# Two shared-expert stages written out without loops, with 7 and 9 chunks in place of 8 and 8, places read directly by GpSimd, and a combination in rings of eight units

## The chip, the cores and the metric

The kernel runs on one core of a Trainium2 chip. The metric is the device time of one execution in microseconds; the table below gives the median of three runs. TensorE multiplies, VectorE and ScalarE work element by element, GpSimd issues the indexed transfers and some small arithmetic, SyncE issues plain transfers.

## What is computed

A layer over x of 4 x 2048 rows of 256 columns: a local attention with 31 taps, then a feed-forward part, each with a layer norm before and after and a residual.

```python
x = x + _layernorm(attn(_layernorm(x)))
y = _layernorm(x)
shared = silu(y @ sg.T) * (y @ su.T) @ sd.T * sigmoid(y @ shared_gate_w.T)     # 704 hidden columns
rw, sel = top_k(softmax(y @ gate_w.T), 2); rw = rw / rw.sum(-1)                # 16 experts
expert_out = sum over the 2 chosen of rw * (silu(g) * h) @ w_down              # 128 hidden columns each
out = x + _layernorm(expert_out + shared)
```

## The kernel before

The 8192 rows are 64 tiles of 128 rows. The program is a row of blocks with a barrier between them.

**Attention and routing** end with scratch tensors in HBM: the normed rows (`yn_scratch`), the same rows turned (`ynt_scratch`), the residual (`x2_scratch`); and in SBUF, for each row, its two places in the list sorted by expert (`slots`), its two shares and the sigmoid of the shared gate (`shgate`). At the end of routing, blocks of `sorted_rows` are cleared by SyncE and ScalarE.

**First shared stage** (`shared_and_scatter`). The shared expert runs over eight chunks of 512 rows (four tiles). A chunk has six steps m, one for each 128 hidden columns (the last has 64). All products are done in three terms of high and low parts. TensorE in step m does `gate_up` (L904) for step m + 2 and `down` (L915) for step m. ScalarE does `silu`: the silu of the gate (L861, waits for gate_up) and then the high part of the hidden values (L863, waits for VectorE). VectorE does `gated` (L886) and `hidden_low` (L891). `split_high` (L855) and `split_low` (L878) cut the chunk's input in two parts; `leave` (L869) brings the four finished tiles out of PSUM. Beside it GpSimd scatters every row to its two places (L984): 128 indexed transfers, 64 rows' tiles by two places, which read `sl`, a copy of a part of `slots` that VectorE makes (L1023). SyncE loads the rows, the transposed chunks (L817), the 16 experts' weights, two a chunk, and stores the shared result (L968). ScalarE and VectorE cut the experts' weights in high and low parts.

**Experts** (`experts`). 144 blocks of 128 sorted rows go through TensorE (L1119 turn, L1143 gate and up, L1150, L1157 down). SyncE loads the blocks (L1096) and stores the results to `expert_rows` (L1101); ahead of its loop it issues four block loads, eight tiny stores (L1106) and the two transposed chunks for the next stage (L817).

**Last stage** (`shared_and_combine`). Eight more chunks of the shared expert. Beside them the 64 tiles are combined in groups of four, in two streams: v = 0 takes the first 32 tiles, whose shared result is loaded back, v = 1 the tiles of the chunk just left. GpSimd gathers the expert rows (L1270, 128 indexed transfers in all). VectorE adds them with their shares and takes the moments (`sums`, L1343, L1347, L1351, L1354). GpSimd makes scale and shift (`scales`, L1277, L1278, L1281 a power, L1283). ScalarE applies them (`centred`, L1301), VectorE adds the residual (`finish`, L1361), SyncE stores (L1254). GpSimd's order is gather(0), gather(1), and then in a loop scales(0, i), gather(0, i + 1), scales(1, i), gather(1, i + 1).

Every engine works in the order of its own program. Waits are on semaphores that another engine counts up.

## Time and profile before

| | us |
|---|---|
| median of 3 runs | 1117.34 |
| lowest and highest | 1115.47, 1120.06 |
| the profiled execution | 1115.37 |
| its span | 1113.6 |

| engine | busy us | share of the span |
|---|---|---|
| TensorE | 950.6 | 85% |
| VectorE | 800.7 | 72% |
| ScalarE | 564.7 | 51% |
| GpSimd | 490.2 | 44% |

In rows of the profile PE is TensorE, DVE VectorE, ACT ScalarE, POOL GpSimd, SPq the queue of SyncE; L904 is line 904 of the kernel before. A row of the timeline is: start in us from the span's start, duration in us, engine, line, operation, out<-in, count, and in brackets the idle time of the engine before it and what ended it. The names of the tiles of the first shared stage begin with `s_`, those of the last with `c`.

### The profile page before, as it was taken

The page shows a single profiled execution, that of the slowest core. Times are in us where ns is not written, and L with a number is a line of the kernel's source. Part 1 is how long each engine was busy: PE and PEld are TensorE (multiplying, and loading weights), DVE is VectorE, ACT ScalarE, POOL GpSimd, SP SyncE. Part 2 cuts the span into 40 slices and gives each one's busy share as a digit, 9 for nine tenths or more (in the row PEclk, how much of TensorE's full clock was granted, in tenths as well). Part 3 has the DMA queues.
Part 4 walks back from the last instruction along what each step waited for, and adds up shares of the span by engine and source line. Part 5 has one row for each costly group of instructions (what it writes and reads, how often), then busy time and mean ns, then how long its engine had stood idle before and what let it go on. Part 6 is the DMA issues. An engine that isn't in the chain of part 4 may idle for free. (4 is left out here: it accounts for less than half of the span.)

```text
span 1113.6 us, 28049 instructions
## 1 busy us (share of the span) xinstructions
PE 950.6 (85%) x9192; PEld 838.9 (75%) x9193; DVE 800.7 (72%) x2066; ACT 564.7 (51%) x1309; POOL 490.2 (44%) x726
## 2 busy tenths in 40 slices
PE   5997898998899407999999589999998899898871
PEld 4787787876788405888888589998998787777761
DVE  5988997797998694444444278887887478777755
ACT  5992456995354313444444345555554345444432
POOL 4413556220555333767776200000000677787774
PEclk9998998999999557999999789999999899999995
DMA  4333688432678527656665345555554556665553
GB/s 137 118 106 92 199 235 263 151 117 65 165 212 248 181 98 242 202 190 208 225 202 180 118 150 170 172 173 175 165 174 151 152 152 189 186 184 168 164 169 109
DMA packets 188966, 188.16 MB, mean 169 GB/s; under 512 B 55120, under 2 KB 169936, under 8 KB 188752
## 3 DMA queue, kind: packets, MB, share of 16 engines
q1 hardware_dynamic: 173088, 149.25, 44.1%
q0 software_dynamic: 12288, 33.57, 9.1%
q10 hardware_dynamic: 3504, 4.20, 1.2%
q8 instruction: 53, 0.87, 0.3%
q14 instruction: 33, 0.27, 0.1%
HBM read 100.81 MB, written 86.14 MB: 168 GB/s over the span
## 5 line engine op out<-in xcount | busy, mean ns | idle before, releaser
L984 POOL DMA_INDIRECT sorted_rows<-yr,sl x128 | 138.1, 1079 | 75.7 <-issue 38.0
L1270 POOL DMA_INDIRECT cy<-expert_rows,csl x128 | 137.9, 1077 | 45.2 <-issue 44.0
L605 PE MATMUL bank<-xbd,am 128*32 128x68 f32 x4096 | 138.2, 304 | 11.2 <-DMA xbd<-xn_scratch 6.8
L605 PEld LDWEIGHTS bank<-xbd,am 128*32 128x32 f32 x4096 | 122.7, 128 | 18.7 <-issue 8.8
L1263 POOL MEMSET czero<- 128x4 f32 x1 | 0.1, 103 | 241.3 <-POOLq L1049 241.3
L886 DVE TENSOR_TENSOR s_hf<-s_sg,bank 128x512 f32<-128x512 f32 (+1 forms) x48 | 33.0, 688 | 89.1 <-ACT s_sg L861 89.1
L1143 PE MATMUL bank<-eh,xh 128*128 x288 | 94.5, 328 | 0.5 <-DVE xl L1187 0.5
L1187 DVE TENSOR_TENSOR xl<-bank,xh 128x256 fp32r<-128x256 f32 x144 | 61.1, 425 | 40.8 <-ACT xh L1169 33.2
L1169 ACT ACTIVATE xh<-bank 128x256 fp32r<-128x256 f32 x144 | 55.4, 385 | 65.3 <-PE bank L1119 64.9
L407 DVE TENSOR_TENSOR am<-probs,mask 128x512 f32<-128x512 f32 x128 | 80.0, 688 | 8.3 <-ACT probs L500 7.4
L1143 PE MATMUL bank<-el,xh 128*128 x288 | 82.3, 286 | 0.0
L1143 PE MATMUL bank<-eh,xl 128*128 x288 | 82.2, 285 | 0.0
L863 ACT ACTIVATE c_hh<-c_hf 128x512 fp32r<-128x512 f32 (+1 forms) x48 | 30.4, 632 | 97.8 <-DVE c_hf L886 97.8
L915 PE MATMUL bank<-dh,c_hh 128*128 128x256 f32 (+1 forms) x192 | 57.1, 297 | 24.7 <-DVE c_hl L891 24.7
L1119 PE MATMUL bank<-ident,xg 128*128 128x128 f32 x288 | 57.2, 282 | 24.4 <-DMA xg<-sorted_rows 12.3
L904 PE MATMUL bank<-c_yh,gh 128*128 128x512 f32 x176 | 72.1, 410 | 6.4 <-DVE c_yl L878 6.4
L514 ACT ACTIVATE av<-av,shift,rstd 128x256 f32<-128x256 f32 x64 | 35.0, 594 | 81.7 <-POOL shift L327 81.7
L322 POOL TENSOR_TENSOR rstd<-mv,eps 128x2 f32<-128x2 f32 (+1 forms) x68 | 14.3, 210 | 138.5 <-DVE mv L397 83.3
L904 PE MATMUL bank<-s_yh,gh 128*128 128x512 f32 x176 | 71.2, 405 | 4.5 <-DVE s_yl L878 4.5
L348 POOL TENSOR_TENSOR x<-av,xr 128x256 f32<-128x256 f32 x64 | 47.0, 755 | 62.8 <-ACT yn L523 59.4
L904 PE MATMUL bank<-c_yl,gh 128*128 128x512 f32 x176 | 70.9, 403 | 0.0
L904 PE MATMUL bank<-c_yh,gl 128*128 128x512 f32 x176 | 70.7, 402 | 0.0
(196 smaller groups left out, 3110.4 us busy)
## 6 DMA issues: line engine op xcount, KB each, us to landing
xg<-sorted_rows SPq DMA_DIRECT2D x144, 128.0 KB, 2.1
expert_rows<-yo SPq DMA_DIRECT2D x144, 128.0 KB, 1.8
xbd<-xn_scratch SPq DMA_DIRECT2D x128, 72.0 KB, 2.3
xt<-xp SPq DMA_DIRECT2D x32, 256.0 KB, 3.0
xn_scratch<-xn SPq DMA_DIRECT2D x64, 128.0 KB, 2.8
xr<-x SPq DMA_DIRECT2D x32, 256.0 KB, 3.6
x_scratch<-x SPq DMA_DIRECT2D x32, 256.0 KB, 3.5
yn_scratch<-yn SPq DMA_DIRECT2D x32, 256.0 KB, 3.5
```

Source lines behind the costliest of these rows:

```text
L348: nc.gpsimd.tensor_tensor(x2[:, q, t], av[:, q, t], xr[:, q, t], ALU.add).then_inc(s["x2_ok"], 1)
L407: nc.vector.tensor_tensor(am[:, q, g], probs[:, bass.ds(i * CB, CB), g, None, :].to_broadcast([P, CB, 2, J]), mask[:, None].to_broadcast([ ...
L514: nc.scalar.activation(av[:, q, t], av[:, q, t], ACT.Identity, scale=rstd2[:, q, t:t + 1], bias=shift2[:, q, t:t + 1]).then_inc(s["z_ok"], 1)
L605: ins = nc.tensor.matmul(pso[q][t][J * b:J * b + J, g * MW:(g + 1) * MW], am[:, q, g, e, side], xbd[:, q, e + side, :, g], start=(g == 0 a ...
L904: ins = self.nc.tensor.matmul(self.pb[2 * k + half][:], w[:, c, col:col + P], y[:, q, c, :], start=(j == 0), stop=(j == 5))
L915: ins = self.nc.tensor.matmul(o, a[0:f, g, t * P:(t + 1) * P], w[0:f, m, :], start=(m == 0 and t % 2 == 0 and j == 0), stop=(m == FT - 1 a ...
L984: nc.gpsimd.indirect_dma_start(out=xg_d, out_offset=bass.IndirectOffsetOnAxis(ap=sl[:, q, t, u, k:k + 1], axis=0), in_=yr[:, t, u], in_off ...
L1119: ins = nc.tensor.transpose(px[r % 2][:, c * P:(c + 1) * P], xg[:, r, c * P:(c + 1) * P], ident[:])
L1143: ins = nc.tensor.matmul(pg[r % 2][:, 0:2 * MF], a[:, r % 2, c * P:(c + 1) * P], w[:, bass.ds(e, 1), c * C:(c + 1) * C], start=(j == 0), s ...
L1169: nc.scalar.activation(xh[:, r % 2], px[r % 2][:, 0:C], ACT.Copy).then_inc(s["xh_ok"], 1)
L1187: nc.vector.tensor_tensor(xl[:, r % 2], px[r % 2][:, 0:C], xh[:, r % 2].bitcast(F32), ALU.subtract).then_inc(s["xl_ok"], 1)
L1270: nc.gpsimd.indirect_dma_start(out=y[:, v, k, j], out_offset=None, in_=yg_d, in_offset=bass.IndirectOffsetOnAxis(ap=sl[:, v, k, j:j + 1], ...
```

## The change

The loops over chunks are written out, so all waits are for constants. The first shared stage takes 7 chunks, the last 9. GpSimd reads `slots` directly for its scatters and gathers; the copies on VectorE are gone. In the first stage SyncE loads two experts and then only rows; ScalarE issues the other experts' loads, the transposed chunks (those of the last stage's first two chunks too) and the stores of the shared result, which the last stage waits for. The low part of the 64 last hidden columns is put into the other half of the high part's tile, below weights that are repeated there, so `down` has two products a tile in place of three in that step.

In the last stage the tiles are combined in 32 units of two tiles. `order` is the sequence of the units, `sums_at` the step of VectorE at which each unit's sums stand: steps 2 to 5 of the first chunk, steps 0, 2, 3 and 5 of the next two, steps 2, 3 and 5 of the rest, and two units behind the last chunk. `centred` stands one step later in ScalarE's program, `finish` two steps later in VectorE's. All buffers of the combination have eight places. GpSimd's sequence is six gathers, then scales and gather in turn.

```diff
+CHUNKS = T // 512
+FIRST = 7
+LATER = CHUNKS - FIRST
...
+        low = self.hl[0:f, g] if m < FT - 1 else self.hh[FL:2 * FL, g]
...
+        terms = ((self.hh, self.dh), (self.hh, self.dl), (self.hl, self.dh))
+        if m == FT - 1:
+            terms = terms[0:2]
...
+            for e in range(2):
+                load_expert(sp, e)
+            for t in range(PAIRS):
+                if t >= R:
+                    sp.wait_ge(s[f"sc_out{t % R}"], t // R * 64)
+                sp.dma_start(yr[:, t % R], yn_d[2 * t:2 * t + 2].rearrange("t p c -> p t c")).then_inc(s[f"yr_in{t % R}"], 16)
...
-                            for k in range(TOPK):
-                                nc.gpsimd.indirect_dma_start(
-                                    out=xg_d, out_offset=bass.IndirectOffsetOnAxis(ap=sl[:, q, t, u, k:k + 1], axis=0),
...
+            for t in range(PAIRS):
+                po.wait_ge(s[f"yr_in{t % R}"], t // R * 16 + 16)
+                for u in range(2):
+                    for k in range(TOPK):
+                        nc.gpsimd.indirect_dma_start(
+                            out=xg_d, out_offset=bass.IndirectOffsetOnAxis(ap=slots[:, 2 * t + u, k:k + 1], axis=0),
+                            in_=yr[:, t % R, u], in_offset=None).then_inc(s[f"sc_out{t % R}"], 16)
...
+            def store(n):
+                act.wait_ge(s["so_ok"], n * 4 + 4)
+                act.dma_start(sh_d[n * 4:n * 4 + 4].rearrange("t p c -> p t c"), so[:]).then_inc(s_kept, 16)
+
+            sh.split_high(act, 0)
+            for n in range(FIRST):
                 for m in range(FT):
...
+                    sh.silu(act, n, m)
+                    if m == 0 and n + 1 < FIRST:
+                        sh.split_high(act, n + 1)
+                    if m == 2 and n > 0:
+                        leave(n - 1)
+                    if m == 4 and n > 0:
+                        store(n - 1)
+                    if m == 4 and n + 2 < CHUNKS:
+                        load_turned(act, sems, yt, ynt_d, n + 2)
+                    if (n, m) in turn:
+                        e = turn.index((n, m))
+                        act.wait_ge(s[f"e_in{e % 2}"], e // 2 * 16 + 16)
+                        nc.scalar.activation(eh[:, e:e + 1], eraw[:, e % 2:e % 2 + 1], ACT.Copy).then_inc(s["e_hi"], 1)
+                    if m % 2 == 1 and m + FT * n > 1 and (e := (m + FT * n + 1) // 2) < E:
+                        load_expert(act, e)
+            leave(FIRST - 1)
+            store(FIRST - 1)
...
-            for q in range(2):
-                load_turned(sp, sems, yt, ynt_d, SHARED_CHUNKS + q, q)
...
+    R, AHEAD = 8, 6
+    EARLY = FIRST * 2
+    MORE = EARLY - 4 - (LATER - 1)
+    order, sums_at, kept = [], {}, 0
+    for n in range(FIRST, CHUNKS):
+        for m in range(2, FT) if n == FIRST else (0, 2, 3, 5) if n - FIRST <= MORE else (2, 3, 5):
+            own = n > FIRST and m in (2, 3)
+            sums_at[n, m] = len(order)
+            order.append((n - 1) * 2 + m - 2 if own else kept)
+            kept += not own
+    order += [(CHUNKS - 1) * 2, (CHUNKS - 1) * 2 + 1]
+    UNITS = len(order)
+    place = {unit: i for i, unit in enumerate(order)}
+    steps = [(n, m) for n in range(FIRST, CHUNKS) for m in range(FT)]
+    finish_at = {steps[k + 2]: sums_at[at] for k, at in enumerate(steps) if at in sums_at and k + 2 < len(steps)}
+    centre_at = {steps[k + 1]: sums_at[at] for k, at in enumerate(steps) if at in sums_at and k + 1 < len(steps)}
...
+            def gather(i):
+                r, unit = i % R, order[i]
+                if i >= R:
+                    po.wait_ge(s["s2_ok"], (i - R) * 2 + 2)
+                for t in range(2):
                     for j in range(TOPK):
...
+                        nc.gpsimd.indirect_dma_start(out=y[:, r, t, j], out_offset=None, in_=yg_d,
+                                                     in_offset=bass.IndirectOffsetOnAxis(ap=slots[:, 2 * unit + t, j:j + 1], axis=0)
+                                                     ).then_inc(s[f"y_in{r}"], 16)
+
+            def scales(i):
+                r = i % R
+                po.wait_ge(s["mv_ok"], i * 2 + 2)
+                nc.gpsimd.tensor_tensor(rstd[:, r], mv[:, r, :, 1], eps[:, 0:2], ALU.add).then_inc(s["var_ok"], 1)
+                nc.gpsimd.tensor_tensor(shift[:, r], zero[:], mv[:, r, :, 0], ALU.subtract).then_inc(s["var_ok"], 1)
+                po.wait_ge(s["var_ok"], i * 2 + 2)
+                nc.gpsimd.tensor_tensor(rstd[:, r], rstd[:, r], neg_half[:, 0:2], ALU.pow).then_inc(s["dev_ok"], 1)
+                po.wait_ge(s["dev_ok"], i + 1)
+                nc.gpsimd.tensor_tensor(shift[:, r], shift[:, r], rstd[:, r], ALU.mult).then_inc(s["norm_ok"], 1)
+            for i in range(UNITS + AHEAD):
+                if i >= AHEAD:
+                    scales(i - AHEAD)
+                if i < UNITS:
+                    gather(i)
...
+            def leave(n):
+                at = [place[2 * n], place[2 * n + 1]]
+                if at[1] >= R:
+                    act.wait_ge(s["o_ok"], (at[1] - R) * 2 + 2)
+                sh.leave(act, n, lambda t: (ff[:, at[t // 2] % R, t % 2:t % 2 + 1], s["so_ok"]))
...
+            sh.split_high(act, FIRST)
+            for n in range(FIRST, CHUNKS):
                 for m in range(FT):
...
+                    sh.silu(act, n, m)
+                    if m == 0 and n + 1 < CHUNKS:
+                        sh.split_high(act, n + 1)
+                    if m == 1 and n > FIRST:
+                        leave(n - 1)
+                    if m == 3 and n + 2 < CHUNKS:
+                        load_turned(act, sems, yt, ynt_d, n + 2)
+                    if (n, m) in centre_at:
+                        centred(centre_at[n, m])
+            left = [i for i in range(UNITS) if i not in centre_at.values()]
+            leave(CHUNKS - 1)
+            for i in left:
+                centred(i)
...
+            def sums(i):
+                r, unit = i % R, order[i]
+                ve.wait_ge(s[f"y_in{r}"], (i // R + 1) * 64)
+                if unit < EARLY:
+                    ve.wait_ge(s[f"in{r}"], loads_of(i) * 16)
+                for t in range(2):
+                    k = 2 * unit + t
+                    if unit >= EARLY:
+                        ve.wait_ge(s["so_ok"], k - 2 * EARLY + 1)
+                    nc.vector.scalar_tensor_tensor(ff[:, r, t], y[:, r, t, 0], share[:, k:k + 1, 0], ff[:, r, t],
+                                                   ALU.mult, ALU.add).then_inc(s["s1_ok"], 1)
+                for t in range(2):
...
+            sh.split_low(ve, FIRST)
+            for n in range(FIRST, CHUNKS):
                 for m in range(FT):
...
+                    sh.gated(ve, n, m)
+                    if m == 1 and n + 1 < CHUNKS:
+                        sh.split_low(ve, n + 1)
+                    if (n, m) in finish_at:
+                        finish(finish_at[n, m])
+                    if (n, m) in sums_at:
+                        sums(sums_at[n, m])
+                    sh.inner_low(ve, n, m)
+            for i in range(UNITS):
+                if i not in finish_at.values() and i not in sums_at.values():
+                    sums(i)
+            for i in range(UNITS):
+                if i not in finish_at.values():
+                    finish(i)
...
-    dn = np.concatenate([i["L0_ffn_shared_w_down"].T, np.zeros((FT * P - FF, C), "f")], 0)
+    dn = np.concatenate([i["L0_ffn_shared_w_down"].T, i["L0_ffn_shared_w_down"].T[FF - FL:]], 0)
```

## Rows read from the trace of the kernel before

**Rows 1.** Stretches: us, busy PE, PEld, DVE, ACT, POOL, PEclk, DMA share, GB/s.
```profile
426.50:623.00 196.50, 196.50 (x1104) 169.46 (x1104) 88.39 (x150) 88.13 (x147) 138.06 (x128) 0.99 0.60 197
...
632.00:860.00 228.00, 210.45 (x1724) 206.01 (x1724) 178.53 (x574) 119.16 (x431) 0.00 (x0) 0.98 0.54 166
...
866.60:1084.00 217.40, 199.62 (x1080) 168.83 (x1080) 156.01 (x390) 97.44 (x182) 164.79 (x204) 0.97 0.56 173
1084.00:1113.60 29.60, 4.64 (x24) 4.13 (x24) 16.50 (x47) 8.18 (x17) 13.62 (x20) 0.60 0.35 110
```

**Rows 2.** The chain that ended last, by line, shares of the span.
```profile
POOL cy L1270 10%; PE bank L904 2%; POOL crstd L1281 2%; POOL crstd L1277 1%; PE bank L915 1%; POOL cshift L1278 0%; ACT cff L1301 0%; DVE cff L1347 0%; POOL cshift L1283 0%; DVE cff L1343 0%; DVE cst L1351 0%; ACT L1296 0%; DVE c_yl L878 0%; ACT c_yh L855 0%; DVE cmv L1354 0%
```

**Rows 3.** Timeline of GpSimd's scatters: first, one at the loop's back edge, last.
```profile
431.33 1.23 POOL L984 DMA_INDIRECT sorted_rows<-yr,sl  x1 [23.48 <-DMA yr<-yn_scratch]
...
476.50 0.97 POOL L984 DMA_INDIRECT sorted_rows<-yr,sl  x1 [2.27 <-DVE sl L1023]
...
619.74 1.90 POOL L984 DMA_INDIRECT sorted_rows<-yr,sl  x1 [0.30 <-issue]
```

**Rows 4.** Waits, first shared stage: total us, times, longest us.
```profile
POOL sorted_rows L984 <- DVE sl L1023: 13.9, 7, 2.3
```

**Rows 5.** The chain in order of time: one step's down products.
```profile
877.38 1.44 PE bank L915 x12
```

**Rows 6.** Timeline: last product of the first shared stage, ScalarE's first act in experts.
```profile
622.85 0.28 PE L915 MATMUL bank<-dh,s_hl 64*128 64x256 f32 x1
...
628.15 1.28 ACT L1165 ACT_TABLE_LOAD   x1 [3.35 <-PEq L936]
```

**Rows 7.** Timeline at the start of the experts: SyncE's queue and TensorE.
```profile
633.96 0.98 SPq L817 DMA_DIRECT2D yt<-ynt_scratch  x2
634.98 3.80 SPq L1096 DMA_DIRECT2D xg<-sorted_rows  x5
...
641.68 0.69 PE L1119 MATMUL bank<-ident,xg 128*128 128x128 f32 x2 [4.99 <-DMA xg<-sorted_rows]
```

**Rows 8.** Stretches behind the hole, columns as in rows 1 (PEclk 1.00 is 2.4 GHz).
```profile
641.70:645.80 4.10, 4.10 (x20) 4.10 (x21) 1.76 (x6) 1.38 (x5) 0.00 (x0) 0.50 0.06 17
```

**Rows 9.** DMA issues: count, KB each, median us to landing.
```profile
xg<-sorted_rows SPq DMA_DIRECT2D x144, 128.0 KB, 2.1
```

**Rows 10.** Groups by line, GpSimd, last stage: busy us, mean ns, idle before.
```profile
L1283 POOL TENSOR_TENSOR cshift<-cshift,crstd 128x4 f32<-128x4 f32 x16 | 4.4, 275 | 1.3
```

**Rows 11.** Timeline of GpSimd, last stage: gathers 1 and 16, period, loop's back edge.
```profile
864.20 1.00 POOL L1270 DMA_INDIRECT cy<-expert_rows,csl  x1 [1.17 <-DVE csl L1329]
...
885.25 0.95 POOL L1270 DMA_INDIRECT cy<-expert_rows,csl  x1 [0.30 <-issue]
...
897.08 1.02 POOL L1270 DMA_INDIRECT cy<-expert_rows,csl  x1 [0.60 <-issue]
...
923.57 0.36 POOL L1277 TENSOR_TENSOR crstd<-cmv,eps 128x2 f32<-128x2 f32 x2
...
1083.43 1.01 POOL L1270 DMA_INDIRECT cy<-expert_rows,csl  x1 [0.55 <-issue]
```

**Rows 12.** Timeline of ScalarE, last stage: silu of step 3, one centred group.
```profile
881.66 0.60 ACT L861 ACTIVATE c_sg<-bank 128x512 f32<-128x512 f32 x1 [2.25 <-PE bank L904]
...
906.05 2.07 ACT L1301 ACTIVATE cff<-cff,cshift,crstd 128x256 f32<-128x256 f32 x4
```

**Rows 13.** Timeline of VectorE, last stage: first sum, low part behind four sums, split.
```profile
887.13 0.88 DVE L1343 SCALAR_TENSOR_TENSOR cff<-cy,share,ckept 128x256 f32<-128x256 f32 x2
...
889.72 0.66 DVE L891 TENSOR_TENSOR c_hl<-c_hf,c_hh 128x512 fp32r<-128x512 f32 x1
...
910.58 1.21 DVE L878 TENSOR_TENSOR c_yl<-yt,c_yh 128x1024 fp32r<-128x1024 f32 x1
```

**Rows 14.** Timeline of the end: first operation of the last scales, last finish.
```profile
1105.45 0.34 POOL L1277 TENSOR_TENSOR crstd<-cmv,eps 128x2 f32<-128x2 f32 x2 [7.58 <-DVE cmv L1354]
...
1108.43 1.80 DVE L1361 TENSOR_TENSOR co<-cff,cx 128x256 f32<-128x256 f32 x4 [3.07 <-ACT cff L1301]
```

More of the change, by code:

```diff
@@ L919, in down, with products @@
             ins.then_inc(self.s["dn_full"], 1)
-    def products(self, pe):
-        def chunk(i, q, first=False, last=False):
-            if first:
-                self.gate_up(pe, i, q, 0)
-                self.gate_up(pe, i, q, 1)
+    def products(self, pe, lo, hi):
+        self.gate_up(pe, lo, 0)
+        self.gate_up(pe, lo, 1)
+        for n in range(lo, hi):
             for m in range(FT):
                 if m + 2 < FT:
-                    self.gate_up(pe, i, q, m + 2)
-                elif not last:
-                    self.gate_up(pe, i + 1, 1 - q, m + 2 - FT)
-                self.down(pe, i, q, m)
-        self.chunks(pe, chunk)
@@ L1034, in _, with expert_low @@
-            chunk(0, 0, first=True)
-            chunk(1, 1)
-            with ve.Fori(0, SHARED_CHUNKS // 2 - 2) as k:
-                chunk(k * 2 + 2, 0)
-                chunk(k * 2 + 3, 1)
-            chunk(SHARED_CHUNKS - 2, 0)
-            chunk(SHARED_CHUNKS - 1, 1, last=True)
+            def expert_low(e):
+                ve.wait_ge(s["e_hi"], e + 1)
+                nc.vector.tensor_tensor(el[:, e:e + 1], eraw[:, e % 2:e % 2 + 1], eh[:, e:e + 1].bitcast(F32),
+                                        ALU.subtract).then_inc(s["e_lo"], 1)
@@ L1042, in _ @@
+            sh.split_low(ve, 0)
+            for n in range(FIRST):
+                for m in range(FT):
+                    sh.gated(ve, n, m)
+                    if m == 2 and n + 1 < FIRST:
+                        sh.split_low(ve, n + 1)
+                    if m % 2 == 0 and 0 <= (e := (m + FT * n) // 2 - 1) < E:
+                        expert_low(e)
+                    sh.inner_low(ve, n, m)
         @block.tensor
         def _(pe):
-            sh.products(pe)
-def experts(nc, sems, eh, el, yt, ynt_d, first_d, xg_d, yg_d, ident, ones, block_expert, pb):
+            sh.products(pe, 0, FIRST)
@@ L1221, in shared_and_combine @@
-        zero = sb("czero", [P, G])
-        names = ["passed", "vpassed", "zeros", "kept_in"] + [f"{n}{v}" for v in range(2) for n in
-                 "sl_ok y_in x2_in s1_ok s2_ok st_ok mv_ok var_ok dev_ok norm_ok z_ok o_ok o_out".split()]
+        y = sb("cy", [P, R, 2, TOPK, C])
+        x2 = sb("cx2", [P, R, 2, C])
+        ff = sb("cff", [P, R, 2, C])
+        st = sb("cst", [P, R, 2, 6])
+        mv = sb("cmv", [P, R, 2, 2])
+        rstd = sb("crstd", [P, R, 2])
+        shift = sb("cshift", [P, R, 2])
@@ L1261, in _ @@
+            for r in range(R):
+                sp.wait_ge(s[f"o_out{r}"], UNITS // R * 16)
         @block.gpsimd
```

408 lines of the change are left out of this document (120 added, 288 removed).

## The prediction, as put on record before the result

> **What bounds the kernel now.** I read the stretches by stage first, then the chain that ended last, then the order of work on GpSimd at each end of the two shared stages. All times are microseconds of the profiled execution. The four lines of [rows 1] are the first shared stage, the experts, the last stage and its end. The shared expert's first stage is TensorE's: busy 196.5 of 196.5 [rows 1]. The experts are TensorE's but for one hole. The last stage is not TensorE's: it works 199.6 of 217.4, and another 29.6 follow in which it does little [rows 1]; the chain there is GpSimd's gathers [rows 2]. So there are three sums to make, and GpSimd's own length must be held against TensorE's in both shared stages.
>
> **First shared stage (8 chunks become 7).** TensorE loses a chunk: 8 chunks last from 426.5 to 623.1, 24.5 each [rows 1, 6]. The last block of hidden columns takes 8 products where it took 12; twelve take 1.44 [rows 5], so 0.5 per chunk goes. TensorE would end at 623.1 - 24.5 - 3.5 = 595. But GpSimd issues all 128 scatters in this stage: from 431.33 to 621.6 [rows 3]. What the change removes is the wait for the copies of places, 13.9 in seven waits of up to 2.3 [rows 4]; less the ordinary gap of 0.30 in each, 11.8. GpSimd then ends at 609.8 if it starts when it did. The first row load, which ends its first wait [rows 3], is now issued behind 0.79 MB of expert weights; at the 197 GB/s of the stage [rows 1] that is up to 4, I take 2, the middle (bounds 0 and 4): 611.8. TensorE is 17 ahead, so this stage is now bound by GpSimd, and the waits moved to ScalarE (expert and transposed loads, the store, which are behind its own casts) have that cover; without it they would cost their issue, some 0.5 each by SyncE's two in 0.98 [rows 7]. Before, the next stage's table load began at 628.15, 6.5 after GpSimd's end, because the last store had to land behind ScalarE's exit copies [rows 6]. Now the landing of a scatter (about 3) ends it: 614.8. **Gain 13.3, bounds 11 and 17.** The skewed queue of SyncE only carries rows now; each pair waits for the scatter four pairs back, which is 20 away, so it costs nothing.
>
> **Experts.** SyncE issued two 512 KB loads at 633.96 ahead of the fifth block's rows at 634.98; TensorE then stood still for 4.99 and ran at half clock from 641.7 to about 645.8 [rows 7, 8]. Both loads leave this queue. At full speed these 4.1 would be 2.1. **Gain 7.0**, bounds 4 (a late landing remains) and 7.5. Nothing takes the hole's place: rows of that size land in 2.1 [rows 9], and the load is issued about 2.7 before it is needed.
>
> **Last stage (8 chunks become 9).** By TensorE alone: one chunk more, 0.5 less in each. It isn't TensorE's stage, so I follow GpSimd. Its order is now: gather units 0 to 5 (four gathers each), then scales(0), gather 6, scales(1), and so on. ScalarE's centred(i) stands one step after sums(i) in ScalarE's own order and waits for scales(i); behind it on ScalarE are all later silu's, on which VectorE and TensorE wait. Call P(i) the time at which scales(i) is done.
>
> P(0): 16 gathers took 864.2 to 886.2, 1.38 each [rows 11]; 24 take 33. Starting at 863.3 (no copy of places to wait for) they end at 896.4, and scales(0) adds 1.4: for four tiles the set took 2.2 (from 1105.45 to 1108.43 less 0.8 of ScalarE and hand-overs [rows 14]), and one addition and one power of 0.7 together go. P(0) = 897.8. ScalarE reaches centred(0) after the silu of step 3, and that step's silu stands at 881.7 [rows 12]. So it stands still for some 14 in the first chunk.
>
> Period of GpSimd: between 897.08 and 1083.43 lie 13 sets of eight gathers and one scales of four tiles, 14.33 each [rows 11]. Two units have the same gathers and powers, one subtraction and one product more (0.28 each, by the product's row [rows 10]), one more pair of semaphore steps (0.15) and one more of the 0.55 gaps in place of 0.30 [rows 11]: 15.1; 0.2 of it were waits that go: 14.9, **7.45 a unit** (bounds 7.1 and 7.7).
>
> Spacing: sums stand at consecutive steps in chunks 8 to 10 in most places, and 7.45 rules there. Where the next sums stand two steps on, the path is centred 1.0 (four took 2.07) and silu 0.6 [rows 12], gated 0.6, finish 0.7, sums 2.6 [rows 13]: 5.5, just below what GpSimd needs for its four gathers (5.5 to 5.9): again 7.45. From the last sums of a chunk (step 5) to the next at step 2 there are three steps: first gated and the high cast of step 0 and the high split delay centred by about 1.2; then centred 1.0, silu 0.6, gated 0.6, low split 1.2 [rows 13], finish 0.7, low cast 0.6, gated 0.6, sums 2.6 = 7.9 (8.2 with the exit copies on ScalarE), then scales 1.4 and 0.2 of hand-overs: 11.0. So chunks with three units take 7.45 + 7.45 + 11.0 = 25.9, above TensorE's 24.
>
> Sum: P(11) = 897.8 + 11 x 7.45 = 979.8. P(12) = 990.8, P(14) = 1005.7, and four more chunks give P(26) = 1109.3. Behind P(26) (at step 0 of the last chunk): to P(27) 11; inner casts, sums 28, centred 27 and 28 to the last block's sums 10.5; last products and exit 2.5; sums of units 30 and 31, 5.5; scales 1.4, centred and finish 1.8, and the store: from the last sums' tiles at 1110.2 to the end at 1113.6 was 3.4 [rows 1, 14]. Together 36: end at 1145.3 instead of 1113.6. **Loss 31.7.** The two tiles per unit in the tail are already in it.
>
> **Total**: -13.3 - 7.0 + 31.7 = +11.4. The profiled execution took 1115.37 for a span of 1113.6 and lies 2 below the median 1117.34; applied to the median, 1128.7. The bounds of the period (21 periods of GpSimd's own) give -7 and +5, those of the first two stages -4 and +6: 1115 to 1141.
>
> **A rule of the Trainium skill against a row.** At the back edge of the scatter loop there is a gap of 2.27 [rows 3], and at that of the combining loop none: its first addition follows the gather at 923.57 without idle time [rows 11]. "Runtime: NRT & Kernel Launch", Instruction fetch mechanics, in the Trainium skill says that a taken branch whose target is out of the two pages held makes the engine wait for a fetch. By the rule, straight-line code would save such a wait at each back edge; the trace agrees for the first loop, and not for the second.
>
> **Rivals.**
> 1. GpSimd runs through. ScalarE's and VectorE's path never holds it, so P(26) = 897.8 + 26 x 7.45 = 1091.5 and the end 1127.5: loss 13.9, total -6.4, 1111. For it: two of three paths come out at or below GpSimd's period. Against: the three-step path is 3 above it. Chance 0.15.
> 2. TensorE rules the last stage. 9 chunks of 24 from 866.6 and 2.4 of slow start give 1085, some 10 of tail, 1095: total -39, 1078. That needs GpSimd to be done with 128 gathers and 32 scales by then, 237 from 863.3, so 1100: against. Chance 0.07.
> 3. Back edges. If GpSimd's loop of the last stage holds waits like the first loop's 2.27 in place of 0.30 [rows 3], hidden in the 14.33 per turn, six go, 12 less than the forecast: 1117. The addition without idle time at 923.57 [rows 11] speaks against. Chance 0.06. This is the rule of the page named above.
> 4. Slower than forecast and than before by another mechanism: TensorE's clock. In chunks 7 to 9 TensorE has 4.0 of work in 7.45. After 5 idle it ran at 1.2 GHz [rows 7, 8]; if it stays there, a step is 8 and rules over 7.45, and each restart lags: half a step (4) in each of three to five chunks, 12 to 20 more, 1144. It decides once a step at the lower clock exceeds GpSimd's period. Against: 4 of work brought the full clock back [rows 8]. Chance 0.10.
> 5. The change doesn't do what it says: scatters don't close up, because their transfers or rows hold them. Then the first stage gains 8 rather than 13.3: 1134. Chance 0.05.
>
> **How the numbers follow.** Forecast 0.57, its own range 1115 to 1141. The range of 8 in 10 takes in most of rivals 1, 3 and 5: 1102 to 1144. A measurement of this kernel tells 0.5%, 5.6, from no change. Faster by over that (under 1111.8): most of rival 1, rival 2, a little of the forecast's low end: 0.22. Within it (to 1122.9): rest of rival 1, rival 3, the forecast's lower part: 0.20. Slower: 0.58.
>
> **What would show it.** In the first stage GpSimd without waits of 2, ending near 611 with TensorE idle from 595; experts without the hole of 5; in the last stage ScalarE waiting some 14 for cshift before its fourth silu of the stage, waits of ScalarE on cshift in all chunks, additions every 7.45 on GpSimd and 11 once a chunk. The prediction is wrong if GpSimd waits for VectorE's moments in the first chunks (then it is ahead, and rival 2 comes near), or if ScalarE's waits on GpSimd are absent.

## Result and the profile after

| | before | after |
|---|---|---|
| median | 1116.62 (4 runs) | 1122.95 (4 runs, 1121.66 to 1125.45) |
| ratio, 95% interval | | 1.0056 (1.0035 to 1.0077) |
| span of the profiled execution | 1113.6 | 1119.9 |
| until ScalarE's table load that opens the experts | 628.15 | 616.95 |
| from there to the table load of the last stage | 234.8 | 234.0 |
| from there to the end | 250.7 | 269.0 |

The changed kernel is slower by 0.6%: small, but its interval leaves out 1. By stage the two profiled executions differ by -11.2, -0.8 and +18.3, together +6.3. The forecast had -13.3, -7.0 and +31.7.

The stretches of the kernel after, with the columns of [rows 1]: the first shared stage, the time until TensorE begins the experts, its first 11.7 there (two lines), the rest of the experts, the last stage and its end.

```profile
424.80:617.00 192.20, 164.44 (x938) 144.80 (x938) 78.43 (x107) 79.31 (x136) 141.40 (x128) 0.93 0.64 206
617.00:619.30 2.30, 0.04 (x1) 0.04 (x1) 0.00 (x0) 1.23 (x1) 0.00 (x0) 0.50 0.47 128
619.30:629.00 9.70, 8.32 (x36) 7.46 (x37) 3.38 (x10) 3.08 (x10) 0.00 (x0) 0.50 0.45 95
629.00:631.00 2.00, 2.00 (x13) 2.00 (x12) 0.94 (x3) 0.83 (x3) 0.00 (x0) 0.63 0.00 0
632.00:850.00 218.00, 200.97 (x1674) 197.64 (x1673) 174.31 (x561) 115.56 (x418) 0.00 (x0) 1.00 0.54 167
850.90:1092.00 241.10, 211.85 (x1124) 178.11 (x1125) 160.56 (x379) 106.99 (x197) 176.22 (x237) 0.96 0.56 164
1092.00:1119.90 27.90, 13.28 (x84) 11.65 (x82) 21.00 (x58) 11.15 (x22) 8.52 (x20) 0.79 0.17 57
```

TensorE is no longer busy throughout the first shared stage (164.4 of 192.2). The timeline there, GpSimd's first and last scatters, TensorE's first act in the experts and the table load, answers [rows 3] and [rows 6]:

```profile
432.85 1.56 POOL L959 DMA_INDIRECT sorted_rows<-yr,slots  x1 [25.27 <-DMA yr<-yn_scratch]
...
612.00 0.96 POOL L959 DMA_INDIRECT sorted_rows<-yr,slots  x1 [0.30 <-issue]
...
616.95 1.28 ACT L1136 ACT_TABLE_LOAD   x1 [24.65 <-PEq L929]
...
619.26 1.15 PE L1090 MATMUL bank<-ident,xg 128*128 128x128 f32 x4 [28.63 <-DMA xg<-sorted_rows]
```

GpSimd ends at 613.0, and TensorE had stopped 28.6 before its next product. The hole of [rows 7] is gone; at the same block TensorE now waits 0.83:

```profile
627.07 0.69 PE L1090 MATMUL bank<-ident,xg 128*128 128x128 f32 x2 [0.83 <-DMA xg<-sorted_rows]
```

The waits of the last stage (us in all, times, longest) show which engine is held up by which:

```profile
ACT c_hh L849 <- DVE c_hf L868: 78.2, 54, 3.5
...
ACT cff L1271 <- POOL cshift L1256: 54.6, 23, 12.2
POOL crstd L1251 <- DVE cmv L1320: 38.6, 12, 8.2
POOL cy L1244 <- issue: 34.9, 127, 0.3
PE bank L888 <- DVE c_hf L868: 17.9, 13, 8.1
```

Before, ScalarE waited for the shift (`cshift`) 10.9 in two waits, and GpSimd for VectorE's moments (`cmv`) 16.2 in three. After, ScalarE waits 54.6 and GpSimd 38.6: each holds the other up. The timeline of the first such wait, ScalarE's silu of step 3 and the first `centred`, and GpSimd's first shift:

```profile
869.64 0.60 ACT L847 ACTIVATE c_sg<-bank 128x512 f32<-128x512 f32 x1 [2.26 <-PE bank L888]
...
883.56 0.20 POOL L1256 TENSOR_TENSOR cshift<-cshift,crstd 128x2 f32<-128x2 f32 x1
...
883.79 1.09 ACT L1271 ACTIVATE cff<-cff,cshift,crstd 128x256 f32<-128x256 f32 x2 [12.17 <-POOL cshift L1256]
```

and, from the fourth chunk on, the scales of the first unit in a chunk with three units:

```profile
971.00 0.54 POOL L1251 TENSOR_TENSOR crstd<-cmv,eps 128x2 f32<-128x2 f32 x1 [3.92 <-DVE cmv L1320]
...
996.03 0.54 POOL L1251 TENSOR_TENSOR crstd<-cmv,eps 128x2 f32<-128x2 f32 x1 [3.92 <-DVE cmv L1320]
...
1021.06 0.54 POOL L1251 TENSOR_TENSOR crstd<-cmv,eps 128x2 f32<-128x2 f32 x1 [3.92 <-DVE cmv L1320]
```

The same wait of 3.92 comes back every 25.03, one chunk of three units. The path behind it goes from the last sums of a chunk (step 5) over three steps to the first of the next (step 2): there a chain that closes on itself sets the pace, and no engine alone. It does not make up all of the 38.6. In the chunks of four units GpSimd waits 0.48 at most and sets the pace itself, a unit every 7.0 to 7.5. Five waits of 2.65 to 3.93 stand at the first unit of chunks of three units (18.3 in all), two of 0.48 ahead of them, and the other 19.3 are five waits at the end, from 1095.30 on.

### The profile page after: what moved, and what is told of

The parts are those of the page before. It is cut to its first block and busy times, and to the rows that moved or that the text cites. A ratio compares the mean times of both kernels' runs of the same rounds, so it can differ in the third digit from the quotient of the medians.

```text
span 1119.9 us, 27085 instructions
## 1 busy us (share of the span) xinstructions
PE 940.7 (84%) x9128; PEld 833.6 (74%) x9129; DVE 796.3 (71%) x2018; ACT 564.6 (50%) x1309; POOL 497.7 (44%) x758
## 3 DMA queue, kind: packets, MB, share of 16 engines
q1 hardware_dynamic: 159120, 131.68, 38.7%
## 5 line engine op out<-in xcount | busy, mean ns | idle before, releaser
L959 POOL DMA_INDIRECT sorted_rows<-yr,slots x128 | 141.4, 1105 | 64.0 <-issue 38.4
L1244 POOL DMA_INDIRECT cy<-expert_rows,slots x128 | 133.8, 1046 | 35.6 <-issue 34.9
L888 PE MATMUL bank<-c_yh,gh 128*128 128x512 f32 x198 | 82.8, 418 | 24.2 <-DVE c_hf L868 17.9
L868 DVE TENSOR_TENSOR c_hf<-c_sg,bank 128x512 f32<-128x512 f32 (+1 forms) x54 | 37.0, 685 | 74.0 <-ACT c_sg L847 73.7
L888 PE MATMUL bank<-c_yl,gh 128*128 128x512 f32 x198 | 80.7, 407 | 0.0
L888 PE MATMUL bank<-c_yh,gl 128*128 128x512 f32 x198 | 80.5, 407 | 0.0
L868 DVE TENSOR_TENSOR s_hf<-s_sg,bank 128x512 f32<-128x512 f32 (+1 forms) x42 | 28.9, 688 | 67.9 <-ACT s_sg L847 67.9
L849 ACT ACTIVATE c_hh<-c_hf 128x512 fp32r<-128x512 f32 (+1 forms) x54 | 34.2, 633 | 78.2 <-DVE c_hf L868 78.2
L1090 PEld LDWEIGHTS bank<-ident,xg 128*128 128x128 f32 x288 | 35.9, 142 | 46.7 <-DMA xg<-sorted_rows 30.1
```

The lines of the kernel that those rows point to most:

```text
L868: self.nc.vector.tensor_tensor(self.hf[0:f, k], self.sg[0:f, k], up, ALU.mult).then_inc(self.s["hf_ok"], 1)
L888: ins = self.nc.tensor.matmul(self.pb[2 * k + half][:], w[:, c, col:col + P], y[:, n % 2, c, :], start=(j == 0), stop=(j == 5))
L959: nc.gpsimd.indirect_dma_start(out=xg_d, out_offset=bass.IndirectOffsetOnAxis(ap=slots[:, 2 * t + u, k:k + 1], axis=0), in_=yr[:, t % R, u ...
L1090: ins = nc.tensor.transpose(px[r % 2][:, c * P:(c + 1) * P], xg[:, r, c * P:(c + 1) * P], ident[:])
L1244: nc.gpsimd.indirect_dma_start(out=y[:, r, t, j], out_offset=None, in_=yg_d, in_offset=bass.IndirectOffsetOnAxis(ap=slots[:, 2 * unit + t, ...
```

## The experiments

All edit the changed kernel. The stages of each profiled execution, cut at the two table loads. In the last stage also three quantities of GpSimd: its waits for `cmv`, the busy time of its 128 gathers, and that of its small operations (`scales`).

| kernel | first | experts | last | waits cmv | gathers | small |
|---|---|---|---|---|---|---|
| before | 628.2 | 234.8 | 250.7 | 16.2 | 137.9 | 43.5 |
| after | 617.0 | 234.0 | 269.0 | 38.6 | 133.8 | 52.3 |
| three ahead | 618.8 | 232.7 | 260.7 | 29.3 | 135.2 | 52.4 |
| later steps | 619.3 | 231.8 | 252.0 | 9.3 | 137.6 | 62.1 |
| later steps, four ahead | 616.0 | 232.4 | 241.2 | 0 | 135.7 | 62.1 |
| 8 and 8 chunks | 620.3 | 230.7 | 255.4 | 26.5 | 132.0 | 52.7 |
| TensorE kept busy | 618.1 | 230.1 | 269.2 | 38.7 | 133.9 | 53.1 |
| loads back on SyncE | 617.2 | 237.0 | 269.7 | 38.6 | 134.4 | 53.1 |
| four ahead | 618.1 | 232.5 | 263.6 | 32.7 | 134.6 | 52.4 |
| later, four ahead, kept busy | 617.7 | 229.7 | 244.2 | 0 | 140.0 | 60.4 |
| the same, 8 and 8 | 636.2 | 230.0 | 233.9 | 0 | 136.2 | 54.5 |
| 8 and 8, later, four ahead | 621.8 | 231.0 | 234.4 | 0 | 136.7 | 54.1 |

Two things are read from it first. The first two stages have the same code after and in three ahead, four ahead, later steps, and later steps with four ahead, and yet the first ends between 616.0 and 619.3 and the experts take 231.8 to 234.0: single executions tell no less than 2 to 3 there. The last stage repeats better: its code is the same after, with TensorE kept busy and with the loads back on SyncE, and it took 269.0, 269.2 and 269.7. And in the last stage the sum of the three GpSimd columns moves as the stage does: from after to the version with later steps and four ahead it falls by 38.6 - 1.9 - 9.8 = 26.9, the stage by 27.8.

### The distance between gathers and scales

```diff
-    R, AHEAD = 8, 6
+    R, AHEAD = 8, 3
```

> The changed kernel with one number changed: GpSimd gathers three units ahead of the scales, not six. Theory A (the order of scales and centred sets the last stage: ScalarE waits in centred for scales, and a chunk of three units is a loop of 25): the first scales are done 12 gathers, not 24, after the stage's start, so about 10 to 15 earlier (VectorE's first moments then come last), and after that the cadence of 25 a chunk stays. The last stage is 10 to 14 shorter, the span near 1108. Theory B (GpSimd's total of gathers and scales is the bound, whatever the order): no change, 1120. Theory C (TensorE's ninth chunk): no change.

The last stage fell by 8.3, less than the 10 to 14 expected. Its waits:

```profile
ACT cff L1271 <- POOL cshift L1256: 43.8, 23, 4.5
...
POOL crstd L1251 <- DVE cmv L1320: 29.3, 11, 4.1
```

The wait of 12.2 is gone, the 23 waits are not: only what stood ahead of the first scales was removed. The scales of the second unit begin 11.8 earlier (877.02, 888.85 after), as expected, and those of unit 27 still 11.5. The rest is lost at the end: what is not gathered ahead at the start has to be gathered there, so that units 27 and 28 are 7.0 apart where they were 3.6 in the version with six ahead. A dose between the two, AHEAD = 4:

> The changed kernel with AHEAD 4 in place of 6 and nothing else; with AHEAD 3 alone the last stage fell by 8.3, with all later steps moved it fell by 17.0, and both together (AHEAD 4) by 27.8. Theory A (only the start counts: ScalarE's wait for the first scales and shift, 12.2 with six units ahead, is what shrinks; every later period is that of the path sums, scales, centred, which doesn't know how far the gathers run ahead): one unit more ahead than in the version with three, so one unit of four gathers, 5, later; the last stage falls by 3 to 6, span 1113 to 1117. Rival B (the gains add up, so AHEAD 4 by itself is worth 27.8 less 17.0): the last stage falls by about 10.8, span 1107 to 1110.

It fell by 5.4, as theory A had it. Two units fewer ahead than in after bring the first `centred` 9.6 earlier (874.21 here, 883.79 after), two units' gathers. The later pace doesn't change: the scales of unit 27 are 9.5 earlier too (1085.77 and 1095.30), and the same 7.0 in place of 3.6 behind them takes most of the difference to 5.4.

```profile
874.21 1.10 ACT L1271 ACTIVATE cff<-cff,cshift,crstd 128x256 f32<-128x256 f32 x2 [2.46 <-POOL cshift L1256]
```

### The distance between sums and centred

`centred` stands five steps behind `sums` in ScalarE's order in place of one, `finish` six in place of two, and the store on SyncE follows two units later.

```diff
-    finish_at = {steps[k + 2]: sums_at[at] for k, at in enumerate(steps) if at in sums_at and k + 2 < len(steps)}
-    centre_at = {steps[k + 1]: sums_at[at] for k, at in enumerate(steps) if at in sums_at and k + 1 < len(steps)}
+    finish_at = {steps[k + 6]: sums_at[at] for k, at in enumerate(steps) if at in sums_at and k + 6 < len(steps)}
+    centre_at = {steps[k + 5]: sums_at[at] for k, at in enumerate(steps) if at in sums_at and k + 5 < len(steps)}
```

> The changed kernel with centred five steps behind the sums instead of one, and finish six instead of two (SyncE's stores lag six units, not four). Order of GpSimd as in the changed kernel. Theory A: the waits of ScalarE for the scales nearly go, the loop of 25 per chunk becomes TensorE's 23.5, GpSimd runs on at 7.15 a unit without waiting for moments; a shift of about 14 stays, since scales lag six gathers. End of the last stage some 20 to 26 earlier: span 1094 to 1100. Theory B: GpSimd's 128 gathers and 32 scales from 851.7 last until 1080 in any order, with a tail of 10: 1090 to 1095 at the least, but it would have been the bound before too, so no gain over 4. Theory C: no change.

The last stage fell by 17.0; 20 to 26 were expected, so the size was missed. GpSimd's wait for the moments fell from 38.6 to 9.3, all of it in the tail, and ScalarE's for the shift from 54.6 to 28.2, of which 26.2 lie ahead of 960:

```profile
ACT cff L1271 <- POOL cshift L1256: 28.2, 10, 4.5
...
POOL crstd L1251 <- DVE cmv L1320: 9.3, 3, 5.4
```

Three terms stand against the gain. The 9.3: with six units gathered ahead, the scales of six are still to come when the last gather is issued, and the last ones wait for VectorE. Then 9.8 went into GpSimd's small operations, which became longer (table: 52.3 to 62.1), and 3.8 into its gathers. The edit moves `centred`, `finish` and the stores together; what each of the three is worth was not measured. With both edits and AHEAD = 4:

> As the run before, and GpSimd gathers four units ahead instead of six. Theory A: both causes of the wait are smaller; TensorE is late by some 5 only, the last chunk ends near 1074, the tail adds 12 to 16: span 1086 to 1092, faster than the kernel before by 2%. Theory B and theory C: as in the run before, no gain to speak of.

Median 1093.65 (1091.28 to 1096.47), ratio to before 0.980 (0.977 to 0.983), span 1089.6 as expected. The last stage fell by 27.8, more than the 17.0 and 5.4 of the parts, and the table shows where: the tail's 9.3 goes only when both are there. That is a reading of two waits, not an experiment of its own. The waits of its last stage have no line of GpSimd for `cmv`, and ScalarE's for the shift are nearly gone:

```profile
ACT cff L1271 <- POOL cshift L1256: 5.8, 5, 2.5
```

GpSimd works from its first gather at 849.13 to the end of its last scales at 1085.36, and its waits for other engines in these 236.2 are 0.6 in all; the rest of its idle time is gaps between its own instructions. Now it is the bound, of a stage of 241.2 in which TensorE is busy for 215.5. Its groups by line:

```profile
L1244 POOL DMA_INDIRECT cy<-expert_rows,slots x128 | 135.7, 1060 | 35.3 <-issue 34.0 <-POOL czero L1235 0.7 <-DVE cff L1313 0.6
...
L1252 POOL TENSOR_TENSOR cshift<-czero,cmv 128x2 f32<-128x2 f32 x32 | 14.6, 457 | 0.0
```

against the subtraction of after, same shape and count:

```profile
L1252 POOL TENSOR_TENSOR cshift<-czero,cmv 128x2 f32<-128x2 f32 x32 | 6.7, 208 | 0.0
```

The timeline shows where a subtraction of 0.2 becomes 1.23 (the version with later steps and four ahead):

```profile
1046.89 0.87 DVE L1308 SCALAR_TENSOR_TENSOR cff<-cy,share,cff 128x256 f32<-128x256 f32 x2
...
1047.38 1.23 POOL L1252 TENSOR_TENSOR cshift<-czero,cmv 128x2 f32<-128x2 f32 x1
...
1047.69 0.87 DVE L1313 SCALAR_TENSOR_TENSOR cff<-cy,share,cff 128x256 f32<-128x256 f32 x2
```

VectorE's four sums end at 1048.56 and GpSimd's subtraction at 1048.61. While each holds the other up, scales run after the sums they wait for; once GpSimd runs freely, its scales can fall beside the sums of another unit. That this accounts for all of the 9.8 is an inference: no run moved the sums away from the scales and changed nothing else. The Trainium skill, "GPSIMD Engine Reference", Specifications, says that GpSimd's access to SBUF is shared with VectorE, with contention where a VectorE instruction has two inputs in SBUF, as these sums have. The rows above agree with it.

### The ninth chunk

```diff
-FIRST = 7
+FIRST = 8
```

> The changed kernel with 8 and 8 chunks, not 7 and 9; nothing else. Theory A: the last stage loses the chunk, but its units now stand four to a chunk, each 7.15 or more of GpSimd's, so only 8 to 13 of the chunk's 25 come off; the first stage's TensorE ends near 616 instead of 592, so it adds 2 to 5. Span 1109 to 1114. Theory C (a ninth chunk of TensorE is the bound): 21 to 25 off the last stage, 3 on the first, span near 1100. The experts' loop shows whether its waits at each pass (15.0 in all, 12.2 in the kernel before) move when code ahead of it grows.

The last stage fell by 13.6, the first grew by 3.3, the span came to 1106.4. Theory C, by which a chunk less is worth the 21 to 25 of TensorE's work, fell. Theory A had the cause right and the size a little low (8 to 13, span 1109 to 1114). With 8 chunks, four units stand in each of the first six and three in the last two. A chunk of four units takes 28.4, GpSimd's own time, with a wait of 0.48 in it; the wait of 3.92 is left once:

```profile
1031.74 0.54 POOL L1251 TENSOR_TENSOR crstd<-cmv,eps 128x2 f32<-128x2 f32 x1 [0.48 <-DVE cmv L1320]
...
1056.77 0.55 POOL L1251 TENSOR_TENSOR crstd<-cmv,eps 128x2 f32<-128x2 f32 x1 [3.92 <-DVE cmv L1320]
```

The 20.2 of waits in the tail stay, and GpSimd's waits for the moments are 26.5 in place of 38.6. So what the ninth chunk cost was not its products, but four more of those waits, since it spreads the same 32 units over more chunks of three. Even with 8 and 8 chunks the new order was slower in the last stage than before, 255.4 against 250.7; only the first stage made that version faster than before.

### The start of the experts

TensorE stood idle for 28.6 before the experts and began them at half clock. 84 products that nobody reads fill some 20 of that time:

```diff
             sh.products(pe, 0, FIRST)
+            pe.wait_ge(sems["hf_ok"], FIRST * FT)
+            for _ in range(84):
+                nc.tensor.matmul(pb[0][:], sh.gh[:, 0, 0:P], sh.yh[:, 0, 0, :], start=True, stop=True)
```

> The changed kernel with 84 products without use behind TensorE's last chunk in the first shared stage, into a bank that the next block overwrites: TensorE works on for about 20 while GpSimd scatters, where it now stands still for 28.6. Nothing else is changed, and no result uses them. If the longer half-clock phase at the start of the experts (from 619.3 to 630.4) comes from this idle time, it is gone or short and the experts start at full clock: 4 to 6 less in the experts, span 1114 to 1116. If the clock is not what was given back, no change in the experts' length of 234.0 (within 1).

Against after the experts took 3.9 less; the span was 1117.4, above the 1114 to 1116 expected. The first product and the stretches at the two clocks:

```profile
620.41 1.11 PE L1093 MATMUL bank<-ident,xg 128*128 128x128 f32 x4 [8.35 <-DMA xg<-sorted_rows]
```

```profile
620.40:627.00 6.60, 6.00 (x27) 5.47 (x27) 2.47 (x7) 2.26 (x7) 0.00 (x0) 0.50 0.39 72
628.00:630.00 2.00, 2.00 (x19) 2.00 (x18) 1.25 (x5) 1.17 (x5) 0.00 (x0) 1.00 0.21 74
```

It ran at half clock (0.50 is 1.2 GHz) for some 7 where after did for 11.2. But the filler is not shown to be the reason. The version with later steps and four ahead had TensorE idle for 27.4, about as long as after, and the full clock was back after 6.7:

```profile
618.30:625.00 6.70, 6.26 (x27) 5.56 (x27) 2.47 (x7) 2.25 (x7) 0.00 (x0) 0.50 0.41 59
625.00:627.00 2.00, 1.65 (x13) 1.37 (x13) 0.81 (x3) 0.92 (x4) 0.00 (x0) 1.00 0.76 257
```

Against the five executions with the same code (mean 232.7) the gain is 2.6, near what single executions can tell.

A later run shows how little the half clock at the start is worth. With 8 and 8 chunks and the filler (below), TensorE was idle for only 2.5 before the experts. Its clock stayed at 1.00, and yet they took 230.0, as much as the 230.1 here. It came sooner to the fifth block and waited longer for its rows:

```profile
638.40:643.10 4.70, 3.98 (x27) 3.19 (x27) 2.39 (x7) 2.14 (x7) 0.00 (x0) 1.00 0.33 59
...
645.68 0.44 PE L1093 MATMUL bank<-ident,xg 128*128 128x128 f32 x2 [2.55 <-DMA xg<-sorted_rows]
```

That is 9.4 behind the table load; after, at half clock up to there, it was 10.1 (627.07 behind 616.95). So up to the fifth block the rows set the pace, and the full clock ahead of it gave back 0.7. Of the 4.0 between the experts of after and of this run, 1.7 more is the half clock behind the fifth block (up to 630.5), and 1.7 are shorter stalls at the back edges of the loop over blocks (15.0 and 13.3).

The filler with the fastest version so far:

> The fastest version so far (AHEAD 4, centred five steps and finish six steps behind sums; span 1089.6) with TensorE kept busy by 84 products more in the idle time before the experts, whose results nobody reads. In it GpSimd has no wait between its first gather at 849 and the last scales at 1085, so a last stage that starts earlier ends earlier by the same. Alone the idle-filling products took 3.9 off the experts and added 1.1 to the first stage. Theory A (the terms of different stages add): span 1086 to 1088, 0.977 of the kernel before. Rival B (what the experts gain is given back in the last stage, since the first chunk there waits for loads and splits as well): span 1089 to 1091.

Median 1092.05 (1091.04 to 1093.27), ratio 0.977 (0.974 to 0.979): the intervals of this and the version without the filler overlap. The experts took 229.7, 2.7 less, and the last stage 3.0 more, since its gathers took 140.0 in place of 135.7. The span, 1091.6, is rival B's; but its cause isn't the one B names, since GpSimd has next to no waits for data in either. The two profiled executions also make the older version look better than it is: the one without the filler is the fastest of its four, this one the slowest. By the medians the filler gained 1.6, which is not clear of the spread of either.

The other half of this term, the loads which the change took off SyncE's queue:

```diff
-                    if m == 4 and n + 2 < CHUNKS:
+                    if m == 4 and n + 2 < FIRST:
...
+            for n in range(2):
+                load_turned(sp, sems, yt, ynt_d, FIRST + n)
             steps(sp, lambda n, r: parts(n, r, (AHEAD, load), (-2, store)))
```

> The changed kernel with the two transposed loads of 512 KB put back where they were, on SyncE ahead of the experts' fifth block. My prediction priced them at 7.0. If the price was right the experts are 7 longer. If half clock hides most of it (TensorE reaches the fifth block at 626.2 now, only 0.8 before its rows), the rows land near 629.5 and TensorE waits 3 to 4 instead of 0.8, and gets its full clock later: 3 to 6 longer.

The experts took 3.0 more than after. The timeline of SyncE and TensorE:

```profile
622.98 0.98 SPq L923 DMA_DIRECT2D yt<-ynt_scratch  x2
...
630.51 0.69 PE L1092 MATMUL bank<-ident,xg 128*128 128x128 f32 x2 [3.95 <-DMA xg<-sorted_rows]
```

The hole of [rows 7] comes back with 3.95 in place of 0.83, and those 3.1 are as large as the difference. Each of the two lengths is a single execution, so the price of the loads is 3 give or take 2, and not the 7.0 of the prediction.

### 8 and 8 chunks with the new order put right

```diff
-FIRST = 7
+FIRST = 8
...
-    R, AHEAD = 8, 6
+    R, AHEAD = 8, 4
```

with the later steps, and at first with the filler too:

> The same as the version with four units ahead, later steps and a busy TensorE, with FIRST 8, so 8 and 8 chunks. Theory A (GpSimd bounds the last stage now: 128 gathers and 32 scales are the same whether 9 or 8 chunks of the shared expert stand beside them): the last stage stays within 3 of 241, the first stage is 3 longer as with 8 and 8 chunks before, experts 230: span 1087 to 1093. Rival B (TensorE bounds the last stage, 24 a chunk): a chunk less takes 20 to 24 off the last stage: span 1066 to 1071.

Median 1101.45, ratio 0.985 (0.983 to 0.987), span 1100.1. The last stage took 233.9. That is 7.3 under the 241.2 that theory A names and 10.3 under the version with 9 chunks and the filler; within 3 was theory A's word, 20 to 24 rival B's, so both sizes are missed and A is the nearer. GpSimd is still without waits, and its own work is shorter: gathers 140.0 to 136.2, small operations 60.4 to 54.5, together 9.7. That a chunk less leaves less of VectorE's work beside them is my explanation, not a measurement. The miss of the span is in the first stage, and it was my own: with 8 chunks TensorE ends only just ahead of the experts, and the filler stood in the way.

```profile
616.75 19.23 PE L1020 MATMUL bank<-s_yh,gh 128*128 128x512 f32 x84
```

Without it:

> 8 and 8 chunks, AHEAD 4, centred five and finish six steps behind sums, without the 84 products. In the run with them TensorE's last product of the first stage ended near 616.8 and they stood behind it for 19.2, 616.75 to 635.98, so that the table load came at 636.24 in place of the 620.29 of the version with 8 and 8 chunks alone; the last stage took 233.9 (from its table load at 866.22 to 1100.1). Theory A (the filling work was itself the delay there, since TensorE has only some 6 of idle time to fill with 8 chunks, and nothing else was lost): first stage to 620, experts 230.7 as with 8 and 8 chunks, last stage 234: span 1083 to 1087, 0.973 of the kernel before. Rival B (GpSimd's last stage is as long as with 9 chunks, 241, and the 7 less were chance): span 1090 to 1093.

Median 1087.75 (1085.99 to 1088.93), ratio 0.973 (0.971 to 0.975), span 1087.2, at theory A's edge. It is the fastest version, 2.7% under the kernel before: first stage 621.8, experts 231.0, last stage 234.4. Without the filler in either, the ninth chunk is worth 241.2 - 234.4 = 6.8 in the last stage.

## Why the prediction was right, and where its steps were not

**Outcome.** Slower was the likeliest case, and the time, 1122.95, lies 5.8 under the forecast of 1128.7, within its own range. But the total is nearer than its parts, and that is luck: the loss in the last stage was 13.4 less than said, the gains were 8.3 less (6.2 in the experts, 2.1 in the first stage), and the two errors have opposite signs. Of the change itself the profiled executions show +6.3 where +11.4 was said.

**First stage: the mechanism held.** -13.3 was said, -11.2 measured. GpSimd started at 432.85, later by 1.5 (2 were taken), and ended at 613.0 (611.8 was said). The waits for copies are gone: its longest is 0.3. The mean scatter took 1.10, where it had taken 1.08; over 128 that is more than the 1.2 by which GpSimd ended late. TensorE is idle from 590.6 on (595 was said). The other mis-sized term is the hand-over, 4.0 for 3. Over the five executions that share this code the mean end is 617.8, a gain of 10.3.

**Experts: the step "nothing takes the hole's place" failed.** 4.2 of the 5.0 came. The rest did not. TensorE's half-clock time was 5.3 at the start and 4.1 behind the hole before [rows 8]. In the changed kernel it ran from 619.3 to 630.5 at 0.50 but for the wait of 0.83, so 10.4 of work at half clock for 9.4: nothing given back, 0.5 lost. And its stall at the back edges of the loop over blocks grew:

```profile
PE bank L1090 <- issue: 15.0, 17, 1.0
```

for 12.2 before in the same 17 places. -4.2 + 0.5 + 2.8 = -0.9, measured -0.8. Over the five executions with this code the mean is 232.7, so 2.1 gained and still far from 7.0. The loop's code is the same; the 17 stalls took 14.6 to 15.6 in all 7-chunk versions without filler, 12.9 and 13.3 with filler, 13.3 to 13.5 with 8 chunks. What sets them wasn't found, and stays open. The prediction was right that the two loads made the hole, wrong that taking them away is worth 7: the run that put them back shows 3.1. Its "Nothing takes the hole's place" left out that the rows behind the hole come late as well: the fifth block's rows let TensorE begin only 10.1 behind the table load.

**Last stage: the mechanism held, its terms were too large.** In the order of the prediction's sum:
- The start of P(0): 24 gathers took 30.6 in place of 33, since a gather with its gap takes 1.27, not the 1.38 of the first sixteen before [rows 11]. P(0) came 883.76 - 850.94 = 32.8 into the stage, not 34.5. ScalarE's 14 of standing still were 12.2.
- The period: 7.1, at the lower bound, for 7.45. (The terms listed for two units, 14.33 + 0.28 + 0.28 + 0.15 + 0.25 - 0.2, make 15.1 and not the 14.9 used, so worked out right it would have been 7.55 and further off.) I carried the 0.55 gap of [rows 11] over to each unit. It is a gap of the loop; the code without a loop has 0.16 in that place, and GpSimd's gaps in all fell from 44.0 to 34.9. P(0) and P(11) are 78.1 apart (883.8 to 961.9), eleven periods of 7.1.
- The three-step path: 11.0 was said for P(11) to P(12), and 11.0 was measured (961.9 to 972.9).
- The chunk: 25.03 for 25.9. Its parts are 11.03 + 7.03 + 6.97, so the difference is in the period again. Four chunks: 3.5.
- The end behind P(26): 32.8 for 36.

**The rivals.** Rival 1, GpSimd runs through, did not happen, and the waits of 3.92 show why; it is what the later steps brought about, with a price it didn't name (9.8 in the small operations). Rival 2, TensorE rules, didn't happen either: it did 225 of work in 269, and a chunk less was worth 13.6 and not its 24. Rival 3: GpSimd in the last stage before had one such wait and not six, and that one stands between two gathers of the loop's last pass, not at its back edge:

```profile
1071.89 0.97 POOL L1270 DMA_INDIRECT cy<-expert_rows,csl  x1 [2.17 <-issue]
```

Rival 4: the clock in the last stage was 0.96 as before (0.97), so half clock did not rule there. Rival 5: the scatters did close up.

**Where the time went, then.** 9 chunks instead of 8 cost the last stage 13.6 and brought the first 3.3. What is left is 4.7 over before at 8 and 8. GpSimd's waits for the moments there are 26.5 against 16.2 (+10.3) and its small operations 52.7 against 43.5 (+9.2; subtraction and product now work on two tiles and not on four, so that there are 128 of them all instead of 96), while it saves 5.9 in gathers and 9.1 in gaps: together +4.5. The waits come from an order in which ScalarE waits for a result of GpSimd one step after its input exists, and from six units gathered ahead: with five steps between and four units ahead the waits are gone, and with 9 chunks 27.8 of the last stage with them. The small operations go with the smaller units, and no run changed those.

## What to carry to other kernels

Where work is woven by hand into a fixed order of several engines, look at each wait which returns at an equal distance: if it comes once per round and each engine in the chain is idle at some time, try a longer distance between producer and consumer in program order before making any operation faster. Here it was worth 17.0 alone and 27.8 with fewer units ahead. Give each such consumer a distance of its own, and keep "how far ahead" just as large as the data needs, since whatever is issued ahead on the same engine stands before the first result and leaves as many results to do at the end. And moving work from a stage bound by one engine to another pays only if the second stage has room in the chain that bounds it, not in the engine that does the work: here a chunk cost 13.6 in one stage and saved 3.3 in the other, and with the order put right it still cost 6.8.

## What was not expected of the hardware

- GpSimd's small operations on 128x2 values depend on what VectorE does beside them: the same 32 subtractions took 0.21 on average after and 0.46 in the version with later steps, singly up to 1.23.
- The half clock at the start of the experts lasted from about 5 to 11.2 behind nearly the same idle time. After and the version with later steps alone both begin behind 28.6 to 28.7 of idle time, and the second is back at full clock 5 after its first product at 621.65:

```profile
621.60:626.00 4.40, 3.86 (x16) 3.23 (x17) 1.26 (x4) 1.43 (x4) 0.00 (x0) 0.50 0.34 64
627.00:629.00 2.00, 0.82 (x8) 0.62 (x7) 1.20 (x4) 0.81 (x4) 0.00 (x0) 1.00 0.78 212
```

  Before, behind 7.3, it was 5.3. So in these executions its length doesn't follow the idle time ahead of it. Whether there is such a phase did: behind 2.5 of idle time the clock stayed at 1.00, behind 6.2 and more it had fallen to 0.50 in every run. The Trainium skill, "TensorE: Matmul & The Clock Gate", Part 1, says that the number of products run at the lower clock varies between runs of one kernel; the traces agree. The page allows the end of this phase half a microsecond either way; 5 to 11.2 is more, and here the measurement decides.
- The rule of "Runtime: NRT & Kernel Launch" in the Trainium skill that was weighed in the prediction is not borne out by the loop of the scatters, where the prediction said that the trace agrees. Its gap of 2.27 comes once a chunk, but the loop is written over pairs of chunks, so three of the six such gaps, this one too, stand where there is no back edge:

```profile
499.75 0.37 DVE L1023 COPY sl<-slots 128x4 uint32 x4
...
500.81 0.97 POOL L984 DMA_INDIRECT sorted_rows<-yr,sl  x1 [2.27 <-DVE sl L1023]
```

  All six scatters begin 1.05 to 1.06 behind the start of VectorE's copies, which is the wait that the row names. So it was the copies that held them, and their going explains the gain without any fetch on GpSimd.
- For the experts' loop over blocks, which stayed a loop, TensorE's stalls grew from 12.2 to 15.0 through a change elsewhere in the program. No run shows why.
